# Attention kernel: normalization on ScalarE and the y transposes moved one head pair earlier

## The chip, the cores and the metric

One Trainium2 chip, all 8 cores, one sequence of the batch per core, the same program on each. The metric is the device time of one execution in microseconds, that of the slowest core.

## What is computed

For each of 8 sequences (2048 tokens, 1024 features) the reference computes one layer: layer norm, then attention and a feed-forward network side by side, both added to the input.

```python
def taylor_exp(x):      # 1, x/RRD, x (x) x / (R2*RD): q.k becomes 1 + s + s*s/2
    x2 = (x[..., :, None] * x[..., None, :]).reshape(..., 256) / R2
    return jnp.concatenate([ones, x / RRD, x2 / RD], axis=-1)
A_qk = jnp.tril(jnp.einsum('bhnd,bhmd->bhnm', taylor_exp(q), taylor_exp(k)))
y    = jnp.einsum('bhnm,bhme->bhne', A_qk, v)            # 16 heads, 64 wide
rms  = jax.lax.rsqrt(jnp.mean(y * y, axis=-1, keepdims=True) + 1e-5)
y    = y * rms * g_weight
out  = x + y_all_heads @ Wo.T + (gelu(xn @ tern(W1).T + b1) @ tern(W2).T + b2)
```

`tern` rounds a weight matrix to -1, 0, 1 by its mean absolute value.

## The kernel before

The program has one hand-written instruction stream per engine (`sync_stream` for SP, `ten_stream` for PE, `vec_stream` for DVE, `sca_stream` for ACT, `gp_stream` for POOL). Each runs in the order written, and semaphores tie them. After layer norm, transposes and the q, k, v projections, attention runs over 8 head pairs, p = 0 to 7, and inside a pair over 16 key tiles m.

Per pair PE opens the four banks of `psY` (L777), waiting for the evacuation of the pair before. It adds the constant part 1/2 + 1/2 of the polynomial with 136 matmuls against `tril05` and `oneh` (L781). Then it computes for each m the scores of both heads in chunks of up to 512 columns into four `psS` banks in turn (L800), and the products with v of the tile before into `psY` (L758). A chunk's polynomial, a square of (score * scale + bias), is made by ACT in one instruction (L646) for two of three chunks and by DVE in two (L465, L469) for the third, into `A_buf`. A new score waits until the chunk four before it has left its bank. The first chunk of a pair is DVE's in pairs 1, 4 and 7 and ACT's in the others.

DVE evacuates `psY` into `y_tm` (L416), a buffer with four slots of one pair each. After the last evacuation of pair p-1, in iteration p, it clears parts of `qh_ext` twice (L446) and makes the sums of squares of pair p-1 in two halves (`rms_vec`, L393 and L396, into `rinv`). ACT takes the root (`rms_sca`, L612). DVE takes the reciprocal and scales the even head of the pair with 16 multiplies (`rms_vec2`, L403, L409). ACT scales the odd head with 16 copies with a scale (`rms_sca2`, L621). SP transposes the finished pair into `yT` by a DMA (L225, L232); a transpose waits for all 16 instructions of both engines, and for the transpose two pairs before.

Which pair is worked on where: DVE's iteration p has `rms_vec(p-1)` and `rms_vec2(p-2)` ahead of its polynomials. ACT's iteration p has `rms_sca(p-2)` and `rms_sca2(p-3)` ahead of its polynomials. SP's iteration p has the copies of q for pair p+1 into `qh_ext` (L217), which wait for the last score of pair p, and then the transpose of pair p-3.

Behind the loop DVE does `rms_vec(7)`, `rms_vec2(6)`, `rms_vec2(7)`. When all eight transposes have landed, POOL loads Wo into `wo_bf` (L281) over the space of `y_tm`, and DVE scales it (L492). PE then runs the output projection (L841), later the two feed-forward stages (L854, L876). W1's conversion on DVE (L501 to L506) comes behind L492 and waits in its second half for the end of the output projection.

Of the kernel before, what the change touches and what calls it, by code (L numbers as in the profile page):

```python
# [27 lines left out]
def strip_chunks(m):  # L28
    t0 = 128 * m
    first_end = 512 * (m // 4) + 512  # L30
    out = [(t0, first_end - t0)]
    b = first_end
    while b < T:
        out.append((b, 512))
        b += 512
    return out


def build_program():
# [77 lines left out]
    def cc(col, n=1):  # L117
        return consts[:, col:col + n]
# [73 lines left out]
    def xt(t):  # L192
        return x_roll[:, t % 6, :]

    def blk(ap2d, nb):
        return ap2d.rearrange("p (b i) -> p b i", b=nb, i=128)

    def sync_stream(e):
        e.dma_start(out=cc(C_G), in_=g_d).then_inc(sG0, 16)
        e.dma_start(out=consts[:, C_B1:C_B1 + 32], in_=b1_d).then_inc(sWb1, 16)  # L200
        for t in range(NT):
            if t >= 6:
                e.wait_ge(sLNu, t - 5)
            dX.inc(e.dma_start(out=xt(t), in_=x_d[t * 128:(t + 1) * 128, :]), t)
        e.wait_ge(sPE, 16)
        for h in (0, 1):
            r0 = 16 * (h % 8)
            e.wait_ge(sQZ, 1)
            e.dma_start(out=qh_ext[r0:r0 + 16, h % 2, :],
                        in_=qT[r0:r0 + 16, h // 8, :]).then_inc(sEXT, 16)  # L210
        for p in range(8):
            for h in (2 * p + 2, 2 * p + 3):
                if h < 16:
                    e.wait_ge(sSC, last_sc_of_pair[p])
                    e.wait_ge(sQZ, 2 * p - 1 if p >= 2 else 1)
                    r0 = 16 * (h % 8)
                    e.dma_start(out=qh_ext[r0:r0 + 16, h % 2, :],  # L217
                                in_=qT[r0:r0 + 16, h // 8, :]).then_inc(sEXT, 16)
            if p >= 3:
                pp = p - 3  # L220
                e.wait_ge(sRMc, NT * (pp + 1))
                e.wait_ge(sRMcS, NT * (pp + 1))
                if pp >= 2:
                    dYTT.wait_done(e, pp - 2)
                dYTT.inc(e.dma_start(out=blk(yT[:, pp, :], NT),  # L225
                                     in_=y_tm[:, pp % 4, :, :],
                                     transpose=True), pp)
        for pp in (5, 6, 7):
            e.wait_ge(sRMc, NT * (pp + 1))
            e.wait_ge(sRMcS, NT * (pp + 1))  # L230
            dYTT.wait_done(e, pp - 2)
            dYTT.inc(e.dma_start(out=blk(yT[:, pp, :], NT),  # L232
                                 in_=y_tm[:, pp % 4, :, :],
                                 transpose=True), pp)
        for t in range(NT):
            e.wait_ge(sWOE, 2 * (t + 1))
            dOUT1.inc(e.dma_start(out=out_d[t * 128:(t + 1) * 128, :],
                                  in_=out_sb[:, t % 2, :]), t)
        for i in range(128):
            tb, j = i // 32, i % 32  # L240
            e.wait_ge(sHGs, i + 1)
            dHGW.inc(e.dma_start(out=hg_scr[j][:, tb * 512:(tb + 1) * 512],
                                 in_=hgst[:, i % 2, :]), i)
        e.wait_ge(sH, 128)
        for k in range(8):
            dHGW.wait_all(e, 32 * (k // 2 + 1))
            if k >= 1:
                e.wait_ge(sO2, 4 * k - 2)
            for part in range(4):
                j0 = part * 8  # L250
                src = bass.AP(hg_scr.tensor, (j0 * 128) * T + 2 * k * 128,
                              [[T, 128], [128 * T, 8], [1, 256]])
                d = e.dma_start(out=hg_ts[:, k % 2, j0:j0 + 8, :], in_=src)
                d.then_inc(dHGR.s[k % 2], 16)
# [303 lines left out]
    def sca_stream(e):  # L558
# [51 lines left out]
        def rms_sca(p):  # L610
            e.wait_ge(sRMa, 2 * (p + 1))
            e.activation(rinv[:, :, 2 * p:2 * p + 2],  # L612
                         rinv[:, :, 2 * p:2 * p + 2], AF.Sqrt,
                         scale=cc(C_CI64), bias=cc(C_CEPS)).then_inc(sRMb, 1)

        def rms_sca2(p):
            e.wait_ge(sRMr, p + 1)
            h = 2 * p + 1
            for t in range(NT):
                sl = y_tm[:, p % 4, t, E:2 * E]  # L620
                e.activation(sl, sl, AF.Copy,  # L621
                             scale=rinv[:, t, h:h + 1]).then_inc(sRMcS, 1)

        for p in range(8):
            if p == 1:
                e.wait_ge(sTHR, 2)
                e.copy(consts[0:1, C_TOT:C_TOT + 2],
                       psY[0:1, 1536:1538]).then_inc(sTHR, 1)
            if p >= 2:
                rms_sca(p - 2)  # L630
            if p >= 3:
                rms_sca2(p - 3)
            for m in range(NT):
                chs = strip_chunks(m)
                for hi in range(2):
                    gs = strip_of[(p, m, hi)]
                    gated = False
                    for ci, (t0, w) in enumerate(chs):
                        idx = poly_idx[(p, m, hi, ci)]
                        if owner[idx] != "S":  # L640
                            continue
                        if gs >= 4 and not gated:
                            e.wait_ge(sAV, gs - 3)
                            gated = True
                        e.wait_ge(sSC, idx + 1)
                        e.activation(A_buf[:, gs % 4, t0:t0 + w],  # L646
                                     psS[idx % 4][:, 0:w], AF.Square,
                                     bias=cc(C_CBI),
                                     scale=cc(C_CSC)).then_inc(sPOLY, 1)
        for p in (6, 7):  # L650
            rms_sca(p)
        for p in (5, 6, 7):
            rms_sca2(p)
        def wo_bank_s(i):
            if i % 4 < 2:
# [227 lines left out]
    with ctx:  # L883
        with nc.Block() as block:
            block.sync(sync_stream)
            block.tensor(ten_stream)
            block.vector(vec_stream)
            block.scalar(sca_stream)
            block.gpsimd(gp_stream)
# [29 lines left out]
```

## Time and profile before

| | us |
|---|---|
| median of the 2 timed runs | 1415.91 (1414.49 to 1417.34) |
| the profiled execution | 1414.61 |
| its span on the slowest core (core 1) | 1412.8 |
| spans of all cores | 1389.9 to 1412.8 |
| busy: PE / PE weight loads / DVE / ACT / POOL | 1000.5 / 517.3 / 562.0 / 538.8 / 80.1 |
| idle of PE between attention and output projection | about 42 |

The attention loop runs from 282 to 741 us, so a pair takes about 57 us. The output projection runs from 783 to 854 us, the feed-forward stages to the end. Times in the trace are microseconds from the start of the span. A row of the timeline merges equal instructions that follow each other: start, length from the first one's start to the last one's end, engine, line, tiles, count, and in brackets the idle time of the engine before it with what ended it.

### The profile page before, as it was taken

Reading aid. Unit: us, or ns where it says so; the run is one execution under the profiler, and the core shown is the slowest. Engines: PE = TensorE matmul, PEld = TensorE weight load, DVE = VectorE, ACT = ScalarE, POOL = GpSimd, SP = SyncE. Lnnn points to the kernel's source line nnn. Section 1 sums busy time; section 2 is a strip of 40 time slices with the busy share of each in tenths; the row PEclk is TensorE's granted clock in tenths of the full one; section 3 lists DMA queues with packets and bytes.
Section 4 is the critical chain, followed back from the end, with each engine's and each line's share of the span. In section 5 each row is a group of like instructions: output and inputs, shape, how many; then the busy total and the mean of one; then the engine's idle time right before and its main releaser. Section 6 shows DMA issues by size and latency. Waiting matters only on the chain.

```text
span 1412.8 us, 21462 instructions; the slowest of 8 cores (1389.9 to 1412.8 us)
## 1 busy us (share of the span) xinstructions
PE 1000.5 (71%) x6824; PEld 517.3 (37%) x6824; DVE 562.0 (40%) x1345; ACT 538.8 (38%) x950; POOL 80.1 (6%) x123
## 2 busy tenths in 40 slices
PE   0011059988788787887870891688799969999996
PEld 0000024455455554564540230233344424444442
DVE  2234410056777777787772636545500000000000
ACT  0455643364747667658563120223233320000000
POOL 1111100000000000000000001111100000001010
PEclk9999999998989989999995896899999989999998
DMA  9787630000000010110106775566622234546652
GB/s 195 255 260 241 228 99 4 1 2 5 2 6 5 2 20 2 20 20 2 35 1 102 241 263 169 171 192 186 199 71 79 75 116 105 134 119 165 163 144 35
DMA packets 96234, 146.12 MB, mean 103 GB/s; under 512 B 22144, under 2 KB 73344, under 8 KB 92032
## 3 DMA queue, kind: packets, MB, share of 16 engines
q0 software_dynamic: 22368, 89.14, 23.2%
q1 hardware_dynamic: 73760, 55.61, 13.2%
q8 instruction: 62, 1.02, 0.3%
q14 instruction: 44, 0.36, 0.1%
HBM read 111.17 MB, written 33.55 MB: 102 GB/s over the span
## 4 chain that ended last, share of the span: by engine, by line
PE 47%; DMA 23%; DVE 12%; issue 9%; ACT 5%; SPq 1%; DVEq 0%; PEld 0%; POOL 0%; ACTq 0%; PEldq 0%; POOLq 0%
PE psS L854 12%; PE psS L876 8%; DMA hg_ts<-hg_scr 7%; DMA p1st<-w1T 6%; PE psS L727 6%; PE psS L800 6%; DMA hg_scr<-hgst 5%; PE psY L758 4%; DVE pv L465 4%; PE psY L781 4%; ACT A_buf L646 3%; DMA p1st<-w2T 3%; PE psS L841 2%; PE psY L841 2%; DVE A_buf L469 2%
## 5 line engine op out<-in xcount | busy, mean ns | idle before, releaser
L646 ACT ACTIVATE A_buf<-psS,consts 128x512 bf16<-128x512 f32 (+3 forms) x427 | 275.9, 713 | 157.4 <-PE psS L800 153.6
L854 PE MATMUL psS<-xnT,w_sb 128*128 128x512 bf16 x1024 | 234.7, 390 | 65.0 <-DVE w_sb L506 39.4
L800 PE MATMUL psS<-qh_ext,kT 128*128 128x512 bf16 (+3 forms) x640 | 171.3, 346 | 65.6 <-DVE A_buf L469 33.5
L465 DVE TENSOR_SCALAR pv<-psS 128x512 bf16<-128x512 f32 (+3 forms) x213 | 129.6, 608 | 154.0 <-PE psS L800 150.8
L854 PEld LDWEIGHTS psS<-xnT,w_sb 128*128 128x128 bf16 x1024 | 100.2, 100 | 199.2 <-issue 91.5
L676 ACT ACTIVATE hgst<-psS,consts 128x512 bf16<-128x512 f32 x128 | 86.7, 686 | 169.6 <-PE psS L854 89.2
L698 PE MATMUL psY<-I,xn_tm 128*128 128x128 bf16 x128 | 14.9, 309 | 181.5 <-ACT xnT L577 131.8
L758 PE MATMUL psY<-v_tm,A_buf 128*128 128x64 bf16 x2176 | 118.2, 192 | 19.1 <-DVE A_buf L480 5.8
L876 PE MATMUL psS<-w2t_sb,hg_ts 128*128 128x512 bf16 x512 | 113.5, 383 | 21.4 <-DMA hg_ts<-hg_scr 21.4
L800 PEld LDWEIGHTS psS<-qh_ext,kT 128*128 128x128 bf16 x640 | 59.8, 96 | 155.3 <-issue 139.6
L758 PEld LDWEIGHTS psY<-v_tm,A_buf 128*128 128x128 bf16 x2176 | 97.7, 96 | 45.2 <-issue 31.6
L532 DVE TENSOR_TENSOR out_sb<-psS,x_re 128x512 f32<-128x512 f32 x16 | 11.1, 692 | 256.7 <-PE psS L876 256.7
L876 PE MATMUL psY<-w2t_sb,hg_ts 128*128 128x512 bf16 x512 | 111.8, 379 | 0.0
L570 ACT ACTIVATE ajunk<-p1st 128x2048 bf16<-128x2048 f32 x32 | 61.2, 1913 | 87.5 <-DMA p1st<-w1T 58.7
L469 DVE TENSOR_TENSOR A_buf<-pv 128x512 bf16<-128x512 bf16 (+3 forms) x213 | 82.1, 385 | 23.3 <-DVE pv L465 1.5
L876 PEld LDWEIGHTS psS<-w2t_sb,hg_ts 128*128 128x128 bf16 x512 | 50.0, 99 | 84.9 <-issue 27.1
L698 PEld LDWEIGHTS psY<-I,xn_tm 128*128 128x128 bf16 x128 | 13.0, 143 | 183.1 <-issue 183.1
L781 PE MATMUL psY<-v_tm,oneh 128*128 128x128 bf16 x960 | 75.9, 246 | 0.0
L781 PEld LDWEIGHTS psY<-v_tm,oneh 128*128 128x128 bf16 x960 | 72.7, 113 | 0.0
L876 PEld LDWEIGHTS psY<-w2t_sb,hg_ts 128*128 128x128 bf16 x512 | 50.0, 98 | 60.5
L841 PE MATMUL psS<-wo_bf,yT 128*128 128x512 bf16 x128 | 32.2, 397 | 42.1 <-DVE wo_bf L492 42.1
L727 PE MATMUL psS<-wv_bf,xnT 128*128 128x512 bf16 x256 | 55.4, 379 | 0.0
(105 smaller groups left out, 788.1 us busy)
## 6 DMA issues: line engine op xcount, KB each, us to landing
p1st<-w1T POOLq DMA_DIRECT2D x16, 1024.0 KB, 7.6
p1st<-w2T POOLq DMA_DIRECT2D x16, 1024.0 KB, 6.2
wst<-w1T POOLq DMA_DIRECT2D x16, 1024.0 KB, 8.3
wst<-w2T POOLq DMA_DIRECT2D x32, 512.0 KB, 4.8
hg_scr<-hgst SPq DMA_DIRECT2D x128, 128.0 KB, 1.8
hg_ts<-hg_scr SPq DMA_DIRECT2D x32, 512.0 KB, 7.9
x_roll<-x SPq DMA_DIRECT2D x16, 512.0 KB, 9.2
out<-out_sb SPq DMA_DIRECT2D x16, 512.0 KB, 4.8
```

The source lines that it names most:

```text
L465: pub(e.tensor_scalar(pv[:, slot, 0:w], psS[idx % 4][:, 0:w], SC, BI, ALU.mult, ALU.add))
L469: e.tensor_tensor(A_buf[:, gs % 4, t0:t0 + w], pv[:, slot, 0:w], pv[:, slot, 0:w], ALU.mult).then_inc(sPOLYV, 1)
L570: e.activation(ajunk[:], p1st[:, i % 2, :], AF.Abs, accum_out=cc(col)).then_inc(sP1R, 1)
L646: e.activation(A_buf[:, gs % 4, t0:t0 + w], psS[idx % 4][:, 0:w], AF.Square, bias=cc(C_CBI), scale=cc(C_CSC)).then_inc(sPOLY, 1)
L676: e.activation(hgst[:, i % 2, :], ps[:], AF.Gelu, bias=consts[:, C_B1 + j:C_B1 + j + 1]).then_inc(sHGs, 1)
L727: mm = e.matmul(ps[:], lhsT, rhs, start=(c == 0), stop=(c == KD - 1))
L758: e.matmul(psY[:, 128 * t + 64 * hi:128 * t + 64 * hi + 64], A_buf[:, gs % 4, 128 * t:128 * (t + 1)], v_tm[:, m, h * E:(h + 1) * E], start ...
L781: e.matmul(psY[:, 128 * t:128 * (t + 1)], tril05[:] if t == mm_ else oneh[:], v_tm[:, mm_, 128 * p:128 * (p + 1)], start=False, stop=False)
L800: e.matmul(psS[idx % 4][:, 0:w], kT[:, h // 8, m * 128:(m + 1) * 128], qh_ext[:, hi, t0:t0 + w], start=True, stop=True).then_inc(sSC, 1)
L841: e.matmul(ps, yT[:, c, t * 128:(t + 1) * 128], wo_bf[:, c, dh * 512:(dh + 1) * 512], start=(c == 0), stop=False)
L854: mm = e.matmul(ps[:], w12_sb[:, c * FF + j * 128:c * FF + j * 128 + 128], xnT[:, 4 * tb:4 * tb + 4, c, :], start=(c == 0), stop=(c == KD ...
L876: mm = e.matmul(ps, hg_ts[:, k % 2, j, (ts % 2) * 128:(ts % 2) * 128 + 128], w2t_sb[:, j, dh * 512:(dh + 1) * 512], start=(j == 0), stop=( ...
```

## The change

ACT's part of the normalization is placed one pair earlier in its stream: iteration p has `rms_sca(p-1)` from p = 1 and `rms_sca2(p-2)` from p = 2. Behind the loop remain `rms_sca(7)`, `rms_sca2(6)` and `rms_sca2(7)`, where `rms_sca(6)`, `rms_sca(7)` and `rms_sca2` of pairs 5, 6 and 7 stood. SP's iteration p has the transpose of pair p-2 from p = 2, and two transposes remain behind the loop instead of three. DVE, PE and POOL are as before.

```diff
@@ sync_stream
-            if p >= 3:
-                pp = p - 3
+            if p >= 2:
+                pp = p - 2
                 e.wait_ge(sRMc, NT * (pp + 1))
                 e.wait_ge(sRMcS, NT * (pp + 1))
@@
-        for pp in (5, 6, 7):
+        for pp in (6, 7):
             e.wait_ge(sRMc, NT * (pp + 1))
             e.wait_ge(sRMcS, NT * (pp + 1))
@@ sca_stream
+            if p >= 1:
+                rms_sca(p - 1)
             if p >= 2:
-                rms_sca(p - 2)
-            if p >= 3:
-                rms_sca2(p - 3)
+                rms_sca2(p - 2)
             for m in range(NT):
@@
+        rms_sca(7)
         for p in (6, 7):
-            rms_sca(p)
-        for p in (5, 6, 7):
             rms_sca2(p)
```

## Rows read from the trace of the kernel before

**Rows 1.** The page's first line.
```profile
span 1412.8 us, 21462 instructions; the slowest of 8 cores (1389.9 to 1412.8 us)
```

**Rows 2.** The chain that ended last, in time: start, us, what.
```profile
744.83 1.23 DVE rinv L396
...
758.12 4.34 DMA yT<-y_tm
...
782.87 3.57 PE psS L841 x8
```

**Rows 3.** Timeline of the tail: start, us, engine, line, tiles, count [idle before <-releaser].
```profile
746.14 0.41 ACT L612 ACTIVATE rinv<-rinv,consts 128x32 f32<-128x32 f32 x1 [6.64 <-DVE rinv L396]
746.46 11.53 ACT L621 ACTIVATE y_tm<-y_tm,rinv 128x64 bf16<-128x64 bf16 x48
748.75 0.34 DVE L403 RECIPROCAL rinv<-rinv 128x32 f32<-128x32 f32 x1
749.21 2.43 DVE L409 TENSOR_SCALAR y_tm<-y_tm,rinv 128x64 bf16<-128x64 bf16 x16
```

**Rows 4.** Timeline of ACT behind its last polynomial of pair 6.
```profile
681.00 3.91 ACT L621 ACTIVATE y_tm<-y_tm,rinv 128x64 bf16<-128x64 bf16 x16
```

**Rows 5.** Timeline at the starts of pairs 1 to 7: last L396, ACT's first polynomials.
```profile
349.90 1.45 ACT L646 ACTIVATE A_buf<-psS,consts 128x512 bf16<-128x512 f32 x2 [11.54 <-PE psS L800]
...
406.07 1.22 DVE L396 TENSOR_REDUCE rinv<-ysq 128x16 f32<-128x1024 bf16 x1
410.24 7.43 ACT L646 ACTIVATE A_buf<-psS,consts 128x512 bf16<-128x512 f32 x11 [15.76 <-PE psS L800]
...
462.25 1.22 DVE L396 TENSOR_REDUCE rinv<-ysq 128x16 f32<-128x1024 bf16 x1
465.56 7.37 ACT L646 ACTIVATE A_buf<-psS,consts 128x512 bf16<-128x512 f32 x11 [9.14 <-PE psS L800]
...
519.10 1.22 DVE L396 TENSOR_REDUCE rinv<-ysq 128x16 f32<-128x1024 bf16 x1
524.87 5.36 ACT L646 ACTIVATE A_buf<-psS,consts 128x512 bf16<-128x512 f32 x8 [0.23 <-PE psS L800]
...
576.96 1.22 DVE L396 TENSOR_REDUCE rinv<-ysq 128x16 f32<-128x1024 bf16 x1
581.07 7.43 ACT L646 ACTIVATE A_buf<-psS,consts 128x512 bf16<-128x512 f32 x11 [9.32 <-PE psS L800]
...
633.45 1.22 DVE L396 TENSOR_REDUCE rinv<-ysq 128x16 f32<-128x1024 bf16 x1
636.50 7.40 ACT L646 ACTIVATE A_buf<-psS,consts 128x512 bf16<-128x512 f32 x11 [8.90 <-PE psS L800]
...
690.38 1.22 DVE L396 TENSOR_REDUCE rinv<-ysq 128x16 f32<-128x1024 bf16 x1
694.17 1.44 ACT L646 ACTIVATE A_buf<-psS,consts 128x512 bf16<-128x512 f32 x2 [9.26 <-PE psS L800]
696.14 5.36 ACT L646 ACTIVATE A_buf<-psS,consts 128x512 bf16<-128x512 f32 x8 [0.52 <-PE psS L800]
```

**Rows 6.** Timeline: PE's fifth score, first AV block, ACT behind (pair 6); PE (pair 7).
```profile
637.42 0.38 PE L800 MATMUL psS<-qh_ext,kT 128*128 128x512 bf16 x1 [0.37 <-ACT A_buf L646]
...
642.87 1.55 PE L758 MATMUL psY<-v_tm,A_buf 128*128 128x64 bf16 x32
...
644.87 1.90 ACT L646 ACTIVATE A_buf<-psS,consts 128x256 bf16<-128x256 f32 x3 [0.96 <-PE psS L800]
...
695.67 0.81 PE L800 MATMUL psS<-qh_ext,kT 128*128 128x512 bf16 x3 [1.16 <-DVE A_buf L469]
```

**Rows 7.** PE in 1-us stretches: stretch, us, busy (count), granted clock, DMA, GB/s.
```profile
624.00:625.00 1.00, 0.84 (x4) 0.50 0.40 66
629.00:630.00 1.00, 1.00 (x12) 0.50 0.00 0
```

**Rows 8.** The same of all engines, in pair 7: PE, PEld, DVE, ACT, POOL, clock, DMA.
```profile
695.00:696.00 1.00, 0.33 (x2) 0.29 (x3) 0.90 (x2) 0.62 (x1) 0.00 (x0) 1.00 0.00 0
```

## The prediction

> **What bounds the kernel now.** I read the page first, for its span [rows 1]: it is the sum to which everything below is added. Then the chain of waits in order of time. The reader is to see in it that the end of the attention is one unbroken chain: the last DVE reduce of pair 7, ACT copying on L621, a DMA transpose that lands, the load of Wo, then PE again on L841 [rows 2]. PE is idle for some 42 us before 782.87 us, and everything after it (output projection, W1 terns, both feed-forward stages) starts relative to that point, so a microsecond won or lost before 782.87 is one at the end. Next comes the timeline of the same stretch, which shows how the ACT part of the chain is made up [rows 3]. Then the timeline at the start of each pair, which shows where ACT and DVE stand when the first scores of the next pair come [rows 4 to 6], and last the granted clock there [rows 7, 8].
>
> At the start of a pair PE runs 4 bank openers and 136 ones/tril matmuls (L777, L781), about 11 us, with no work for ACT's polynomials. Before, ACT uses that hole for the normalization work of older pairs: its 16 copies of L621 begin at 681.00, right behind its last polynomial of pair 6, take 3.91 us, and ACT then sits idle 9.26 us until the first score of pair 7 [rows 4, 5]. From that first score on, the order turns round: ACT runs 10 or 11 polynomials of 512 columns with no gap, 7.37 to 7.43 us for 11 of them, and PE, which has only four psS banks, is paced by them [rows 5]. In pair 6 PE reaches its first block of AV matmuls at 642.87, just ahead of the end of ACT's burst at 643.90; only after that block does ACT wait for PE (0.96 us) [rows 6]. So ACT's burst is on the path at the start of each pair, and PE on the path through the rest of it.
>
> **The change part by part.**
> *Moved work, in number.* Nothing is added or removed. ACT still has 8 instructions of L612 and 128 of L621, DVE its 8 reciprocals and 128 multiplies, SP its 8 transposes. ACT's L612 is one pair earlier, L621 one pair earlier, the transpose one pair earlier.
>
> *The tail.* Before, three batches of L621 (pairs 5, 6, 7) sit behind the last L612, which waits 6.64 us for DVE's reduces of pair 7: 48 instructions in 11.53 us, a pitch of 0.24 us [rows 3]. After, pair 5's batch is done at the start of pair 7, and 32 remain. That takes 16 x 0.238 = 3.81 us out. Is something else late next? Pair 7's batch needs the reciprocal, which ends at 748.75 + 0.34 = 749.09; ACT gets to that batch at 746.46 + 3.81 = 750.27, so it does not wait. DVE's multiplies of pair 7 end at 749.21 + 2.43 = 751.64, ACT's copies at 757.99 - 3.81 = 754.18, so ACT stays last. SP's transposes go from three to two; the last is issued at about 754.3 instead of 758.12 and lands 4.34 us later as before, and Wo's load follows [rows 2, 3]. Gain: 3.81 us, all of it on the chain.
>
> *The start of pairs 2 to 7: the new wait.* In iteration p ACT now runs L612 for pair p-1, which waits for DVE's second reduce (L396) of pair p-1. DVE makes that only after it has evacuated pair p-1 and cleared qh_ext twice. Behind L612 on ACT's queue stand the 16 copies of L621 and then all polynomials of the pair. When does ACT get free? In the tail the pitch behind this wait is visible: L396 starts at 744.83, L612 at 746.14 (+1.31), L621 at 746.46 (+0.32) [rows 2, 3]. L621's own new wait, for the reciprocal of pair p-2, ends in the same moment: DVE issues it right behind L396, as in the tail. With 16 pitches of 0.238 us = 3.81 us, the first polynomial can start at (start of the last L396) + 1.31 + 0.32 + 3.81 = + 5.44 us. Against the first polynomial of before [rows 5], pair by pair:
> pair 2: 406.07 + 5.44 = 411.51, was 410.24: late by 1.27;
> pair 3: 462.25 + 5.44 = 467.69, was 465.56: 2.13;
> pair 5: 576.96 + 5.44 = 582.40, was 581.07: 1.33;
> pair 6: 633.45 + 5.44 = 638.89, was 636.50: 2.39.
> In pairs 4 and 7 the first chunk is DVE's, and ACT had a gap after two polynomials. What counts there is the end of the burst: ten at a pitch of 0.66 us, the last 0.77 long, are 6.71 us. Pair 4: 519.10 + 5.44 + 6.71 = 531.25, was 524.87 + 5.36 = 530.23: 1.02. Pair 7: 690.38 + 5.44 + 6.71 = 702.53, was 696.14 + 5.36 = 701.50: 1.03.
> Sum: 1.27 + 2.13 + 1.02 + 1.33 + 2.39 + 1.03 = 9.17 us. Bounds: zero, if what follows the burst takes it up, and 9.17, if nothing does. I take 9.17. ACT paces PE through the first 10 or 11 polynomials, and once PE is late, ACT's later waits are for PE, not spare time of PE.
>
> *Pair 1.* Only L612 for pair 0 comes in, in a hole of 11.54 us [rows 5]. It would end 1.31 + 0.40 us after the last L396 starts; even in pair 6, where DVE is latest, that is 635.16, ahead of the first polynomial at 636.50. Cost nothing; the cover is PE's ones block, and without it the 0.4 us would count.
>
> *SP.* In each iteration the transposes stand behind the two qh_ext copies of that iteration and hold back nothing but each other. Moved one pair earlier, the one of pair 5 waits at the start of pair 7 for ACT's copies (about 695.8 us) and has the whole pair to land. y_tm's buffers come free one pair earlier, and DVE never waited for them. DVE's reciprocals wait for L612 of a pair that is a whole pair old. All of this costs nothing; if the covering pair were gone, a transpose would cost its 4.34 us.
>
> *Sum.* 9.17 - 3.81 = +5.4 us. The profiled execution took 1414.61 us (span 1412.8, the rest around it), which makes 1420.0. It lies 1.30 us under the median 1415.91 of the runs shown, so I forecast 1415.91 + 5.4 = 1421.3.
>
> **The rivals.**
> *A. The late start is taken up, and the tail gain shows.* For it: right behind the first AV block ACT waits 0.96 us for PE, so it has spare time in a pair, and in pair 7 PE's fifth score waits for DVE, not for ACT [rows 6]. Against it: ACT runs 11 without a gap [rows 5] and PE depends on it through four banks. It decides as soon as less than 3.8 of the 9.2 us persist. At full effect: 1415.9 - 3.8 = 1412.1.
> *B. The longer PE hole drops the clock.* After four scores PE must wait for ACT's first polynomial. In pair 6 that hole was 0.37 us [rows 6] and becomes 0.37 + 2.39 = 2.76 us; in pair 3 2.50 us. At the end of pair 5 the granted clock falls to 0.50 of full (1.2 GHz) from 624 to 630 us, behind a stretch in which PE had short gaps, and it is at 1.00 (2.4 GHz) in the burst, where PE is busy only 0.33 of a slice [rows 7, 8]. Should such a stretch start anew in the burst, PE's work in it takes twice as long: at most half of some 6.6 us = 3.3 us each, less what ACT's pace hides. In pairs 3 and 6 alone +6.6, at 1428; in all six +20, at 1441 (+1.8%), the slow end. Against it: pair 7 has a hole of 1.16 us here already and keeps 1.00 [rows 6, 8].
> The Trainium skill, "TensorE: Matmul & The Clock Gate", section "Why this matters for your kernels", warns that an idle gap of PE between bursts of matmuls sends it back to half clock; the trace of before shows falls at pairs' ends and none in the burst, and no run yet shows a hole of 2.8 us there. By that rule the time would be that of rival B's smaller case at most; by the row of pair 7 it stays the forecast's.
> *C. The tail does not shrink* because Wo's load or its neighbours set the time instead: 1415.9 + 9.2 = 1425.1. Against it: POOL's only unmet wait there is for the transposes, and the chain runs through ACT without a gap.
>
> **How the numbers follow.** Forecast 0.62, with its own range 1417 to 1426 (terms half as large or a third larger, and 1.4 us either way between executions). A 0.17, B 0.13, C 0.06, others 0.02. The range of 8 in 10 runs from A's full value, 1412, to B's smaller case, 1428. Two per cent, 28 us, is about what a measurement of this kernel can tell from no change. All cases but the extreme of B together with something unforeseen stay within it: same 0.95, slower 0.03, faster 0.02.
>
> **What would show it.** In the changed kernel: a wait of ACT's L612 for DVE's L396 in every pair, some 6 to 8 us each; ACT's idle time before its first polynomial near zero in pairs 2 to 7, where it was 9 us; L621's second appearance ending at +5.4 us from L396's start; PE waiting up to 2.8 us behind its first four scores with ACT named as releaser; pair starts drifting by a growing 1.3, 3.4, 4.4, 5.8, 8.1, 9.2 us; 32 instead of 48 copies in the tail, and 3.8 us less between PE's last AV work and L841. Wrong if the pairs keep their old length (A), if the granted clock reads 0.50 within ten us of a pair's first score (B), or if L841 starts as long after the last AV as before (C).

## The result

The changed kernel is slower by 0.43 per cent: the ratio to the kernel before is 1.0043 with a 95% interval of 1.0029 to 1.0057, medians 1423.9 against 1416.07 us in the same sessions. The medians are over all executions, the ratio over undisturbed ones. By the ratio that is 6.1 us, with 4.1 to 8.1 as its interval. The forecast was 5.4 us more (1421.3), inside 2 per cent.

The page's first line and the waits of ACT's L612, which the page's slowest core (now core 5) shows:

```profile
span 1414.3 us, 21462 instructions; the slowest of 8 cores (1402.1 to 1414.3 us)
```
```profile
L612 ACT ACTIVATE rinv<-rinv,consts x8: 416/418/420, 351.4 to 763.0; 128x32 f32<-128x32 f32 x8
its engine sat idle before it (us, times) until:
  DVE rinv L396: 83.0, 8
```

Before, one of the eight roots waited, 6.64 us in the tail [rows 3]. Now all eight do, 7.2 to 13.2 us each, 10.4 in the mean. The span of one execution (1414.3 against 1412.8) says little about 6 us: the eight cores of one execution lie 12 to 23 us apart, and their order changes from execution to execution. The stages tell more. The next table gives means over the eight cores of one profiled execution of each kernel. A pair is measured from PE's first opener (L777, now L776) to the next pair's; pair 7 to the start of DVE's last L396; the tail from there to PE's first L841 (now L840). The output projection is taken from its first to its last L841, the row below it from there to the first L854.

```
us, mean of 8 cores     before    after   difference   forecast
pair 1                   60.21    60.21      0.00        0
pair 2                   55.71    57.24     +1.53      +1.27
pair 3                   57.01    59.18     +2.17      +2.13
pair 4                   58.40    59.58     +1.18      +1.02
pair 5                   56.19    57.58     +1.39      +1.33
pair 6                   56.91    59.60     +2.69      +2.39
pair 7                   63.04    64.41     +1.37      +1.03
tail                     38.32    35.01     -3.31      -3.81
attention to L841       501.7    508.7      +7.0       +5.4
output projection        70.0     70.0
projection to L854       40.2     39.6
L854, first to last     251.8    252.1
L876, first to last     230.8    230.2
```

Up to L841 the stages add 7.0 us, and the four rows behind it give about 1 us of that back. The tail's row is the loose one: it differs by up to 4.5 us between the cores of one execution, a pair's by 1.6 at most.

Here is the start of pair 6 in the changed kernel, by engine. It answers to the row of pair 6 in [rows 5] and to [rows 6]. Timeline rows: start, us, engine, line, tiles, count, idle before.

```profile
645.50 1.22 DVE L396 TENSOR_REDUCE rinv<-ysq 128x16 f32<-128x1024 bf16 x1
646.64 0.34 DVE L403 RECIPROCAL rinv<-rinv 128x32 f32<-128x32 f32 x1
...
646.82 0.42 ACT L612 ACTIVATE rinv<-rinv,consts 128x32 f32<-128x32 f32 x1 [11.24 <-DVE rinv L396]
647.14 3.94 ACT L621 ACTIVATE y_tm<-y_tm,rinv 128x64 bf16<-128x64 bf16 x16
650.98 4.13 ACT L646 ACTIVATE A_buf<-psS,consts 128x512 bf16<-128x512 f32 x6
655.29 3.38 ACT L646 ACTIVATE A_buf<-psS,consts 128x512 bf16<-128x512 f32 x5 [0.18 <-PE psS L799]
...
647.95 1.03 PE L799 MATMUL psS<-qh_ext,kT 128*128 128x512 bf16 x4
651.88 0.38 PE L799 MATMUL psS<-qh_ext,kT 128*128 128x512 bf16 x1 [2.90 <-ACT A_buf L646]
...
657.64 1.55 PE L757 MATMUL psY<-v_tm,A_buf 128*128 128x64 bf16 x32
```

The first polynomial starts 5.48 us behind the start of the last L396 (5.44 was reckoned). PE's scores have been there since 648; PE stands for 2.90 us behind the fourth and names ACT. In the kernel before the copies lay in the hole ahead of the scores [rows 4]. The chain that ended last now goes through them. This is its part at the start of pair 2:

```profile
411.39 1.23 DVE rinv L396
412.71 0.21 ACT rinv L612
...
413.03 1.11 ACT y_tm L621 x5
...
414.23 1.12 ACT y_tm L621 x5
...
416.15 0.81 ACT y_tm L621 x3
416.96 2.01 ACT A_buf L646 x3
```

The tail answers to [rows 2, 3]: the timeline of ACT and POOL, then the end of the chain.

```profile
762.96 0.42 ACT L612 ACTIVATE rinv<-rinv,consts 128x32 f32<-128x32 f32 x1 [7.22 <-DVE rinv L396]
763.28 7.77 ACT L621 ACTIVATE y_tm<-y_tm,rinv 128x64 bf16<-128x64 bf16 x32
...
776.03 0.88 POOL L281 DMA_DIRECT2D wo_bf<-woT  x1 [583.12 <-DMA yT<-y_tm]
```
```profile
763.28 7.78 ACT y_tm L621 x32
...
771.18 4.31 DMA yT<-y_tm
...
776.91 16.37 DMA b_bf<-b2r
...
796.78 3.57 PE psS L840 x8
```

32 copies take 7.77 us instead of 48 in 11.53, a gain of 3.76. Behind them the transpose took 4.31 us (4.34 before), and the load of Wo with the small load behind it, the chain's DMA row, 16.37 (15.51 on the core shown before).

One thing is new, the granted clock in pair 6's burst, which here means PE's work from the pair's first score to its first AV block (PE in 1-us stretches: stretch, us, busy (count), granted clock, DMA, GB/s):

```profile
649.00:650.00 1.00, 0.00 (x0) 1.00 0.00 0
650.00:651.00 1.00, 0.00 (x0) 1.00 0.00 0
651.00:652.00 1.00, 0.12 (x1) 1.00 0.00 0
652.00:653.00 1.00, 0.71 (x3) 0.65 0.00 0
653.00:654.00 1.00, 1.00 (x4) 0.50 0.00 0
654.00:655.00 1.00, 0.75 (x3) 0.50 0.00 0
655.00:656.00 1.00, 1.00 (x4) 0.65 0.00 0
656.00:657.00 1.00, 0.62 (x3) 1.00 0.00 0
```

Behind two slices of idle PE the clock is at 0.50 (1.2 GHz) for 3.4 us in sum. In the kernel before it read 1.00 in pair 6's burst on all eight cores, as in pair 7's [rows 8].

### The profile page after: what moved, and what is told of

The parts are those of the page before. It is cut to its first block, busy times and chain, and to the rows that moved or that the text cites. A ratio compares the mean times of both kernels' runs of the same rounds, so it can differ in the third digit from the quotient of the medians.

```text
span 1414.3 us, 21462 instructions; the slowest of 8 cores (1402.1 to 1414.3 us)
## 1 busy us (share of the span) xinstructions
PE 1001.1 (71%) x6824; PEld 516.0 (36%) x6824; DVE 562.8 (40%) x1345; ACT 541.8 (38%) x950; POOL 78.7 (6%) x123
## 4 chain that ended last, share of the span: by engine, by line
PE 46%; DMA 25%; DVE 11%; issue 8%; ACT 7%; SPq 1%; DVEq 0%; POOL 0%; PEld 0%; ACTq 0%; PEldq 0%; POOLq 0%
PE psS L853 10%; PE psS L875 8%; DMA p1st<-w1T 7%; PE psS L799 7%; DMA hg_scr<-hgst 6%; PE psS L726 6%; DMA hg_ts<-hg_scr 6%; PE psY L757 5%; DVE pv L465 4%; DMA p1st<-w2T 3%; ACT A_buf L646 3%; PE psY L780 2%; PE psS L840 2%; PE psY L840 2%; PE psY L875 2%
## 5 line engine op out<-in xcount | busy, mean ns | idle before, releaser
L853 PE MATMUL psS<-xnT,w_sb 128*128 128x512 bf16 x1024 | 228.2, 381 | 60.7 <-DVE w_sb L506 38.7
L799 PE MATMUL psS<-qh_ext,kT 128*128 128x512 bf16 (+3 forms) x640 | 178.2, 361 | 71.7 <-DVE A_buf L469 31.9
L840 PE MATMUL psS<-wo_bf,yT 128*128 128x512 bf16 x128 | 32.9, 403 | 39.5 <-DVE wo_bf L492 39.5
```

What stands on the lines that cost most here:

```text
L799: e.matmul(psS[idx % 4][:, 0:w], kT[:, h // 8, m * 128:(m + 1) * 128], qh_ext[:, hi, t0:t0 + w], start=True, stop=True).then_inc(sSC, 1)
L840: e.matmul(ps, yT[:, c, t * 128:(t + 1) * 128], wo_bf[:, c, dh * 512:(dh + 1) * 512], start=(c == 0), stop=False)
L853: mm = e.matmul(ps[:], w12_sb[:, c * FF + j * 128:c * FF + j * 128 + 128], xnT[:, 4 * tb:4 * tb + 4, c, :], start=(c == 0), stop=(c == KD ...
```

## The experiments

In all of them the pairs and the tail are measured as in the table above, and the diffs are excerpts: `...` marks what is left out. The theory is that of the forecast: the cost is the 16 copies of L621 that stand behind a wait for DVE, and the gain is 16 copies less in the tail. The rival readings were that the wait itself, whatever stands behind it, is what costs; that the transposes or the load of Wo make the tail; and, for the part of the cost above the reckoned sum, that it is the clock.

**1. The root alone, one pair earlier, behind the copies.**

```diff
-            if p >= 2:
-                rms_sca(p - 2)
             if p >= 3:
                 rms_sca2(p - 3)
+            if p >= 1:
+                rms_sca(p - 1)
...
-        for p in (6, 7):
-            rms_sca(p)
+        rms_sca(7)
```

> Of the change only the root (rms_sca) is one pair earlier, and it stands behind the 16 copies of rms_sca2(p-3), not ahead of them; the tail keeps its 48 copies. Theory (the cost is the 16 copies that are held back until the wait is over): the copies run in ACT's hole, the root's 0.4 us ends before the first polynomial, so the pairs keep their lengths within 0.2 us and the time is that of before (ratio 1.000). Rival (waiting for DVE at the start of a pair is itself what costs): pairs 2 to 7 grow by 1 to 2 us each as in the changed kernel, ratio about 1.007.

Measured: ratio 0.9997 (0.9968 to 1.0026). Pairs 2 to 7: 55.71, 56.95, 58.28, 55.93, 56.95, 63.05, within 0.3 us of before each; tail 38.30 against 38.32. ACT waits for DVE with every root, 6.8 to 13.2 us on the two cores read (0 and 5), and it costs nothing: only the root's 0.4 us stands between the wait's end and the pair's first polynomial.

**2. The wait ahead of the copies, the tail as before.**

```diff
-            if p >= 2:
-                rms_sca(p - 2)
+            if p >= 1:
+                rms_sca(p - 1)
             if p >= 3:
                 rms_sca2(p - 3)
...
-        for p in (6, 7):
-            rms_sca(p)
+        rms_sca(7)
```

> ACT waits with the root of pair p-1 first and then makes the copies of pair p-3 (so 16 copies behind the wait in pairs 3 to 7, none in pair 2); the tail keeps its 48 copies and three transposes. Theory: pair 2 keeps its length of before, pairs 3 to 7 grow as in the changed kernel (2.3, 1.2, 1.3, 2.7, 1.4 us, about 9 in all), nothing comes back in the tail: ratio about 1.0065, 2 to 3 us slower than the changed kernel less pair 2's 1.5. Rival (the tail's gain is not real, or the reciprocal's wait is the one that costs): the time of the changed kernel less 1.5, or of before.

Measured: ratio 1.0053 (1.0026 to 1.0081). Pair 2, which has no copies here, is 55.69 against 55.71. Pairs 3 to 7 grow by 2.18, 1.44, 1.05, 2.39 and 1.51, in sum 8.6. The tail is 39.1, not shorter. The same two groups of instructions as in experiment 1 and in the same pair, only their order turned round, make the difference between nothing and 8.6 us by the stages (7.5 by the ratio).

**3. The tail's gain with one late pair.**

```diff
             if p >= 3:
                 rms_sca2(p - 3)
+            if p == 7:
+                rms_sca(6)
+                rms_sca2(5)
...
-        for p in (6, 7):
-            rms_sca(p)
-        for p in (5, 6, 7):
+        rms_sca(7)
+        for p in (6, 7):
             rms_sca2(p)
```

> ACT's iterations 1 to 6 are those of before; in iteration 7 the root of pair 6 and the copies of pair 5 are added behind those of pair 4, and the tail has 32 copies and, on SP, three transposes of which one is ready early. Theory: only pair 7 pays (about 1.0 to 1.7 us), the stretch from DVE's last reduce to the output projection shrinks by 3.8 us: net 2 to 3 us faster, ratio 0.998. Rival (the gain in the tail is given back by the load of Wo or a transpose): that stretch shrinks by less than 1 us and the ratio is 1.001.

Measured: ratio 0.9981 (0.9960 to 1.0003). Pair 7 grows by 1.46, the pairs before it by 0.1 at most, the tail is 34.89, 3.4 us shorter. Net of the stages 2.0 us; the ratio says 2.7, and its interval touches no change. The stages decide here, and SP's three transposes behind the loop were no hindrance.

**4. The reciprocal first.** DVE's part of pair p-2 goes ahead of the two clears and the sums of squares, and ACT's copies of pair p-2 need nothing else.

```diff
@@ vec_stream
+            if p >= 2:
+                rms_vec2(p - 2)
             if p >= 1:
                 (two clears of qh_ext)
                 rms_vec(p - 1)
-            if p >= 2:
-                rms_vec2(p - 2)
@@ sca_stream, against the changed kernel
-            if p >= 1:
-                rms_sca(p - 1)
             if p >= 2:
+                rms_sca(p - 2)
                 rms_sca2(p - 2)
...
-        rms_sca(7)
+        for p in (6, 7):
+            rms_sca(p)
```

> The changed kernel with DVE's reciprocal and multiplies of pair p-2 ahead of its two clears of qh_ext and its sums of squares, and ACT's root back where it was: ACT's copies of pair p-2 wait only for a reciprocal that comes 0.4 us behind the last evacuation. Theory: ACT is free 4 to 5 us before the first score of a pair, pairs 1 to 7 keep their lengths of before within 0.3 us, and the tail still has 32 copies: 3.8 us faster than before, ratio 0.997. Rival (the clears, now 2.9 us later, hold back the scores, or DVE itself was the late one): pairs grow by 1 to 3 us and the ratio is 1.000 or more.

Measured: ratio 0.9972 (0.9950 to 0.9994). Pairs 2 to 7 are 55.83, 56.84, 58.43, 55.84, 56.91, 63.03: in sum 0.4 us less than before. The tail is 35.45, 2.9 us shorter: ACT's copies in it take 3.8 us less, and the stretch from Wo's issue to DVE's L492 took 0.7 us more in this execution. Timeline at the start of its pair 6, on its slowest core:

```profile
624.96 0.40 ACT L612 ACTIVATE rinv<-rinv,consts 128x32 f32<-128x32 f32 x1
628.09 3.92 ACT L621 ACTIVATE y_tm<-y_tm,rinv 128x64 bf16<-128x64 bf16 x16 [2.73 <-DVE rinv L403]
...
626.54 1.92 PE L776 MATMUL psY<-v_tm,zrow_bf 1*128 1x512 bf16 x4
...
637.58 1.03 PE L799 MATMUL psS<-qh_ext,kT 128*128 128x512 bf16 x4
...
644.48 1.51 PE L757 MATMUL psY<-v_tm,A_buf 128*128 128x64 bf16 x32
```

ACT still waits for DVE, 2.73 us, but it is done with its copies at 632.0, 5.6 us ahead of the first score. From first score to first AV block PE takes 6.90 us, as before. So the change's idea was sound, and what was against it was that its waits end behind DVE's sums of squares: with the reciprocal ahead of them the tail's copies are saved and the pairs cost nothing. The edit also puts the root back to where it was before the change; experiment 1 shows that its place alone costs nothing behind the copies.

**5. Pair 6 out of the tail too.** On top of experiment 4, in iteration 7 the root of pair 6 stands behind m = 3 and two copies (ACT, shown) and two multiplies (DVE, left out of the excerpt) of pair 6 behind each m from 8 to 15; none of it is left behind the loop.

```diff
@@ sca_stream, end of each m
+                if p == 7 and m == 3:
+                    rms_sca(6)
+                if p == 7 and m >= 8:
+                    rms_sca2(6, range(2 * m - 16, 2 * m - 14))
```

> As recip_first, and pair 6's scaling is taken out of the tail into pair 7: the root behind m = 3, two copies of ACT and two multiplies of DVE behind each m from 8 to 15. The tail has 16 copies and 16 multiplies. Theory: the stretch from the last reduce to the output projection is 7.6 us shorter than before; pair 7 grows by at most 3.8 us (the copies' time on ACT), likely 1 to 2, since ACT and DVE wait for PE there: 5.5 us faster than before in the middle, ratio 0.996. Rival (anything put into the ring of scores and polynomials costs in full): pair 7 grows by 3.8 or more and it is no better than recip_first, 0.997.

Measured: ratio 0.9956 (0.9933 to 0.9979). Pair 7 is 63.97 (+0.9), the tail 30.78 (-7.5). The 3.8 us of ACT's and 2.4 of DVE's work that went into pair 7 cost 0.9 us there: most of it, near a pair's end and in small pieces, must lie in time that both engines wait for PE, which is argued and not shown. It tends to be better than experiment 4 (0.9956 against 0.9972), by less than the intervals can part; the stages part them.

**6. The hole of PE filled.** In the changed kernel PE gets 8 matmuls of a zero tile behind the fourth score of pairs 2 to 7; they add zeros. PE also waits once, ahead of the attention, for the zero tile.

```diff
+                        if p >= 2 and m == 0 and hi == 0 and ci == 3:
+                            for _ in range(8):
+                                e.matmul(psY[:, 0:512], zlhs[:],
+                                         v_tm[:, 0, 0:512],
+                                         start=False, stop=False)
```

> The changed kernel with 8 matmuls of an all-zero weight tile (128x512, adding zeros to an open psY bank) behind the fourth score of pairs 2 to 7, where PE otherwise has a hole of 1.6 to 2.9 us. Theory: the cost is ACT's late start (9.2 us over six pairs by the sum, 11 to 12 as measured), and the 2 us between these come from the granted clock, which falls to half behind the hole: with the hole filled the clock stays at 1.00 in the burst and each burst (first score to first AV block) shortens to its length of before plus ACT's lateness, pair 6 from 9.7 to about 9.2 us, pair 5 from 9.1 to about 7.9. Rival (the surplus has another cause, such as DVE's polynomials being late): bursts keep 9.7 and 9.1 us.

Measured: ratio 1.0013 (0.9987 to 1.0040). Pairs 2 to 7: 57.15, 58.82, 59.45, 56.96, 59.26, 64.04, in sum 1.9 us less than in the changed kernel, for 48 matmuls more. From its pair 6 on its slowest core, timeline and 1-us stretches of PE:

```profile
643.72 1.89 PE L806 MATMUL psY<-v_tm,zlhs 128*128 128x512 bf16 x8
645.94 0.38 PE L800 MATMUL psS<-qh_ext,kT 128*128 128x512 bf16 x1 [0.32 <-ACT A_buf L646]
...
645.03 7.34 ACT L646 ACTIVATE A_buf<-psS,consts 128x512 bf16<-128x512 f32 x11
```
```profile
645.00:646.00 1.00, 0.68 (x4) 1.00 0.00 0
...
648.00:649.00 1.00, 0.80 (x3) 1.00 0.00 0
```

Low stretches of the granted clock in the 16 us from the first score, in the four cores I read (0, 2, 5, 7) and pairs 2 to 7, so 24 bursts: before, a low stretch of 3.4 us in 2 of them (both in pair 2); in the changed kernel in 21, in one of them twice; with the filler in none. Over all eight cores it is 3 of 48 (all in pair 2), 44 of 48 and none; in experiments 1 and 4, which have no long hole, 2 of 48 each. From first score to first AV block: pair 6 had 6.82 us before (mean of the four), 9.26 in the changed kernel and 8.43 with the filler. Pair 5 had 6.40, 8.68 and 8.27. So the falls come with the hole, all but the few of pair 2. My numbers for the bursts were too high for pair 6 (I had expected 9.2) and too low for pair 5 (7.9). On the whole time the clock's part is 1.9 us by the stages and 4 us by the ratios, whose intervals overlap. The filler has a price that I did not separate: 1.89 us of matmuls in holes some of which are shorter. ACT's own rows settle most of it. ACT's first 11 polynomials of a pair (10 in pairs 4 and 7), from the first one's start to the last one's end, mean of eight cores:

```
us                  pair 2  pair 3  pair 4  pair 5  pair 6  pair 7
changed kernel        7.66    7.68    6.98    7.66    7.65    6.97
with the filler       7.41    7.34    6.75    7.41    7.34    6.74
```

The differences add up to 1.6 of the 1.9 us. The four bursts of the changed kernel that saw no fall (pair 2 on core 1, pair 3 on core 2, pair 7 on cores 0 and 2) have the filler's lengths: 7.41, 7.34, 6.75 and 6.74. So a fall costs about 0.3 us a burst, by holding up ACT's polynomials.

**7. SP's part undone.** Transposes of pair p-3 in the loop and three behind it, all else as changed.

> The changed kernel with SP's part undone: transposes one pair later again and three behind the loop. Theory: where the transpose stands costs and gains nothing, since pair 5's is ready and issued before the tail's two are; the same time as the changed kernel, ratio about 1.004, and the stretch from last reduce to output projection as in it. Rival (the tail's gain comes from the transposes): that stretch is 3 us longer than in the changed kernel.

Measured: ratio 1.0046 (1.0023 to 1.0069); pairs within 0.2 us of the changed kernel's; tail 34.6 against 35.0. The diff's lines in `sync_stream` neither cost nor gain.

**8. The rest of the tail's chain.** Experiment 5 with Wo loaded early into a free buffer. In the trace that load is issued at 188 to 199 us, before the attention starts, not during it. The first loads of W1 follow on the same queue and no longer wait behind Wo's; they now wait for DVE's last reduce, since their buffer (`wst`) overlaps `ysq`.

```diff
@@ gp_stream
-        dYTT.wait_all(e, KD)
-        e.dma_start(out=wo_bf[:], in_=...)
+        e.wait_ge(sP1R, 32)
+        e.dma_start(out=wo_st[:], in_=...)        # 16 KB free since the weight statistics
...
         e.wait_ge(sYE, 128)
+        e.wait_ge(sRMa, 16)                       # then the loads of W1
@@ vec_stream
         e.wait_ge(sWOG, 32)
+        dYTT.wait_all(e, KD)
-            e.tensor_scalar(wo_bf[:, c, :], wo_bf[:, c, :], cc(C_G), ...
+            e.tensor_scalar(wo_bf[:, c, :], wo_st[:, c, :], cc(C_G), ...
...
+        e.wait_ge(sWOGs, KD)
```

> As pair6_inside, and Wo is loaded during the attention into a free 16 KB buffer (where the first weight statistics had lain); when all transposes have landed, DVE scales it from there into wo_bf, so the load is no longer behind the transposes. Theory (the stretch from DVE's last reduce to the output projection is one chain, and every link of it counts in full): of the chain's links, POOL's issue and the load of 15 to 16 us go, DVE's scaling and the transposes stay, so the stretch shrinks from 31 to about 15 us and the kernel is about 22 us faster than before in all, ratio 0.984. Rival (what follows, W1's conversion and its loads, is what sets the start of the feed-forward stage): the stretch shrinks but the gain is given back before the feed-forward stage, ratio 0.996 as pair6_inside.

Measured: ratio 0.9809 (0.9769 to 0.9849), 27 us faster than before, the best of all. The tail is 15.65 us. The stages account for 22.2 us (479.5 from the attention's start to the projection, 501.7 before). Behind the tail little was given back: projection 70.5, then 39.9 to the first matmul of the feed-forward stage, 251.3 for that stage and 233.0 for the last (2.2 more than before). That leaves 20 us by the stages of one execution, just under the ratio's interval of 21 to 33 us, which rests on few executions; how much more than 20 it is stays open. Its chain in the tail, slowest core:

```profile
748.61 1.23 DVE rinv L398
750.88 3.93 ACT y_tm L627 x16
754.93 6.58 DMA yT<-y_tm
761.61 3.27 DVE wo_bf L497 x8
765.01 3.57 PE psS L848 x8
```

One link grew: the last transpose takes 6.58 us where it took 4.3 (from its issue to DVE's scaling it is 5.5 to 6.7 us over the cores). The first loads of W1 now start at 750.41, beside it, instead of behind Wo's, a likely cause that I did not test.

## Why the prediction was right

*Where the path lies.* Every stage behind L841 has its length of before within 0.7 us in the changed kernel, and experiment 8 took 22 us from before the projection and kept at least 20 of them at the end. That the start of the projection carries everything behind it holds.

*The tail.* The reckoned 3.81 us for 16 copies was 3.76 on the slowest core and 3.81 in the mean of the cores (11.54 to 7.73), and the stretch shrank by 3.31. The rest is two small terms: the root starts 1.59 us behind L396's start where it was 1.32, on every core, for a reason that no run shows, and from Wo's issue to DVE's first L492 it took 16.91 us instead of 16.68. That last one is no effect of the change: it lies anywhere from 15.0 to 18.4 us on the cores of one execution of the kernel before. SP and DVE were indeed free (experiment 7).

*The wait at the pairs' starts.* The pitch of 5.44 us from L396 to the first polynomial was 5.48. The order of the pairs came out as reckoned, pair 6 the dearest and pairs 4 and 7 the cheapest (only pairs 2 and 5 changed places), and with 9.17 expected the six pairs cost 10.33. The choice of the upper bound, that nothing behind the burst takes the lateness up, was right: experiment 2 shows it without the tail's gain, and experiment 1 shows that it is not the wait as such. The pairs' starts drifted by 1.5, 3.7, 4.9, 6.3, 9.0 and 10.3 us against the listed 1.3 to 9.2. The waits of L612 in pairs 1 to 7 were 7.7 to 13.2 us, longer than the 6 to 8 given as a sign; only their end is in the sum, so this changed nothing.

*The term that was too small.* 1.2 us of 10.3 were missing from the sum. I had kept the fall of the clock (rival B) apart, as something that happens or does not, with 6.6 to 20 us at stake and with pair 7's hole of 1.16 us as evidence against it. It happens in nearly every burst of the changed kernel: of the prediction's own signs of being wrong, the clock at 0.50 within ten us of a pair's first score came true in 44 of 48 bursts. The forecast had this mechanism wrong and kept its number because a fall is cheap here. It lasts 3.4 us, not 6.6 (6.8 in 3 of the 44), and costs 0.3 us, a tenth of what rival B put on it, since most of it lies under ACT's pace, which still sets PE's. There is some luck in the size as well: without the falls the six pairs cost 8.4 us at most (the filler's run), less than the 9.17 reckoned, and the two errors partly cancel.

Pair 7 of before was thin evidence: there a hole of 1.1 to 1.3 us with one of 0.3 behind it kept 1.00 on all eight cores, but on core 5 of the changed kernel a fall follows a hole of 0.99 and one of 0.72 us. Nor was the burst of before free of falls, as the row of one core had it: pair 2 had one on three of eight cores. The Trainium skill, "TensorE: Matmul & The Clock Gate", section "Why this matters for your kernels", warns of long idle gaps between bursts of matmuls. The trace fits that behind the hole of 2.90 us (clock 0.50 at 653), but falls came behind shorter holes as well.

*The range.* Its two ends do not follow from one rule: the lower, 1417, has the net sum halved and 1.4 us taken off, while the upper, 1426, needs the pairs' term alone a third larger; with both terms a third larger it is 1424.5. Nothing hangs on it, since the measured +6.1 us lies well inside.

*The others.* Rival A (taken up) fell with the length of each of pairs 2 to 7. Rival C (no gain in the tail) fell with experiment 3. The forecast of +5.4 us lies inside the measured interval, 4.1 to 8.1; the stages of one execution say +7.0 up to L841, 1.2 of it from the pairs and 0.5 from the tail beyond the sum.

What stays open: why pair 3 has bursts 1 us longer on some cores than on others with the filler and without, how the 4 us of experiment 6's ratio divide between the clock and chance, and why the tail's root comes 0.27 us later.

## What to carry to other kernels

Work moved ahead of a loop on an in-order engine costs what stands behind its last wait, not what it takes: before moving it, look where in its new place the producer ends, and order the producer's own queue so that the one result that is waited for comes first. A wait ahead of 0.4 us of work was free here, the same wait ahead of 3.8 us cost 1 to 2.7 us at each of six places, and with DVE's reciprocal moved up it was free again. When a chain of single links separates two stages, look at its longest link first: the copies were 3.8 us of a stretch in which a load of 15 us, which needed nothing from the attention but its space, could be moved out whole.

## What was unexpected of the hardware

In the changed kernel PE has a hole of 0.8 to 3.1 us behind a pair's first scores, and the granted clock fell to 0.50, for 3.4 us as a rule, in 44 of 48 such bursts. Eight matmuls of an all-zero tile in that hole (1.89 us) kept it at 1.00 in all 48. The length of one hole does not tell whether the clock falls: behind 1.1 to 1.3 us it stayed at 1.00 in pair 7 of the kernel before, and in pair 4 of the changed kernel it fell on all eight cores behind 0.8 to 1.2 us with 0.6 to 0.7 us following. A fall cost only about 0.3 us a burst, seen in ACT's row: its 11 polynomials took 7.6 to 7.8 us with a fall and 7.3 to 7.4 without.
